# Input terms and weight splits beside the first recurrence tile, weight maxima beside the second attention

## The reference, cut to what matters

```
x = x + attn(cond(x, cond_2048, Wq, Wk, Wv, b), Wq2, Wk2, Wv2, Wo)
gi = x @ W_ih + b_ih                       # input terms of all 256 rows
for each row t:                            # h starts as cond_2048, 8 x 512
    gh = h @ W_hh + b_hh
    r, z = sigmoid(i_r + h_r), sigmoid(i_z + h_z)
    n = tanh(i_n + r * h_n)
    h = (1 - z) * n + z * h
...
h1 = silu(einsum('td,ehd->teh', hs, w1) + b1)      # 8 experts, 352 hidden
out = einsum('ted,te->td', einsum('teh,edh->ted', h1, w2) + b2, comb)
x = x + out
```

## Time and profile before

| | |
|---|---|
| median of 3 runs | 2149.39 us (2143.58 to 2150.28) |
| the profiled execution | 2148.9 us |
| its span, first to last instruction | 2146.8 us |
| TensorE matmul, weight load busy | 1933.3 us (90%), 1687.2 us (79%) |
| VectorE, ScalarE, GpSimd busy | 1346.2 us (63%), 936.4 us (44%), 115.5 us (5%) |
| mean granted TensorE clock | 0.947 |

### The profile page before, as it was taken

How to read it: one execution, slowest core, us unless ns; L and a number is a source line. 1 busy time by engine, 2 the same in 40 slices (tenths; PEclk the granted TensorE clock), 3 DMA queues, 4 the chain that set the end, 5 groups by cost and what they waited for, 6 DMA issues and landing times.

```text
span 2146.8 us, 82157 instructions
## 1 busy us (share of the span) xinstructions
PE 1933.3 (90%) x34302; PEld 1687.2 (79%) x34302; DVE 1346.2 (63%) x5134; ACT 936.4 (44%) x3370; POOL 115.5 (5%) x189
## 2 busy tenths in 40 slices
PE   5889989989998695976689999999999999999999
PEld 3677677677675574866579989989899899898998
DVE  4566665665666107955567776676767766767664
ACT  1355445545545221223335444455454444554443
POOL 0021021021011220000000000000000000000000
PEclk9999999999999897986679999999999999999999
DMA  6000000000000471220000000000000000000000
GB/s 259 1 1 0 0 0 0 0 0 0 0 0 2 152 254 57 74 72 12 9 18 18 18 13 18 18 28 4 28 18 18 13 18 18 28 4 28 4 13 11
DMA packets 54435, 66.14 MB, mean 31 GB/s; under 512 B 4928, under 2 KB 46272, under 8 KB 53104
## 3 DMA queue, kind: packets, MB, share of 16 engines
q1 hardware_dynamic: 50608, 46.96, 6.5%
q0 software_dynamic: 3520, 14.69, 2.2%
HBM read 44.83 MB, written 16.81 MB: 29 GB/s over the span
## 4 chain that ended last, share of the span: by engine, by line
PE 46%; DVE 7%; issue 2%; ACT 1%; DMA 0%; DVEq 0%; ACTq 0%
PE ps L1339 26%; PE ps L1294 10%; PE ps L1273 10%; DVE dh L1470 1%; ACT nn L1390 1%; DVE hn L1463 1%; DVE dh L1476 1%; DVE nxt L1479 1%; DVE nxt L1482 1%; DVE tn L1447 1%; DVE rn L1459 1%; PE ps L1326 0%; DVE h L1480 0%; DVE ns L1472 0%; DVE tb L1556 0%
## 5 line engine op out<-in xcount | busy, mean ns | idle before, releaser
L1339 PE MATMUL ps<-nxt,whf 128*128 128x32 f16 x24576 | 660.5, 177 | 79.3 <-DVE nxt L1482 73.2
L1339 PEld LDWEIGHTS ps<-nxt,whf 128*128 128x128 f16 x24576 | 650.7, 96 | 99.4 <-DVE nxt L1482 88.2
L1390 ACT ACTIVATE rz<-s,sc 128x32 f32<-128x32 f32 x512 | 164.7, 322 | 469.0 <-DVE s L1447 467.8
L1273 PE MATMUL ps<-cur,w1f 128*128 128x256 f16 x2112 | 274.0, 275 | 0.0
L1294 PE MATMUL ps<-hh,w2f 128*128 128x256 f16 x2112 | 265.8, 273 | 0.0
L1294 PEld LDWEIGHTS ps<-hh,w2f 128*128 128x128 f16 x2112 | 205.6, 98 | 23.7
L1447 DVE TENSOR_REDUCE s<-ps 128x32 f32<-128x64 f32 x512 | 114.9, 224 | 165.5 <-PE ps L1339 163.3
L1273 PEld LDWEIGHTS ps<-cur,w1f 128*128 128x128 f16 x2112 | 199.5, 98 | 23.1
L965 PE MATMUL ps<-x1T,wi 128*128 x768 | 175.6, 392 | 21.4 <-DMA wi<-in_W_ih 14.1
L965 PEld LDWEIGHTS ps<-x1T,wi 128*128 128x128 f32 x768 | 150.5, 197 | 46.2 <-issue 24.0
L471 PE MATMUL ps<-kz,rot 128*128 128x256 f32 x512 | 158.0, 391 | 0.0
(11 more groups left out here) (205 smaller groups left out, 2811.2 us busy)
## 6 DMA issues: line engine op xcount, KB each, us to landing
gi_d<-stage SPq DMA_DIRECT2D x96, 128.0 KB, 1.7
gi<-gi_d SPq DMA_DIRECT2D x16, 768.0 KB, 4.9
w1f<-in_w1T POOLq DMA_DIRECT2D x4, 1408.0 KB, 8.7
xall<-in_x SPq DMA_DIRECT2D x4, 1024.0 KB, 9.1
x1T<-in_xT SPq DMA_DIRECT2D x1, 4096.0 KB, 21.9
w2f<-in_w2T POOLq DMA_DIRECT2D x8, 512.0 KB, 4.6
out<-x1T SPq DMA_DIRECT2D x8, 512.0 KB, 3.2
wi<-in_W_ih SPq DMA_DIRECT2D x1, 3072.0 KB, 11.9
```

The costliest lines, as they stand in the source:

```text
L1273: last = nc.tensor.matmul(ps[:, 6 + n % 2, 0:TT], w[:, wp, i % NHC * P:(i % NHC + 1) * P], cur[:, k, hq, :, :].rearrange("p s b -> p (s b) ...
L1339: last = nc.tensor.matmul(ps[:, bank, g * WIDE * 2 * B:(g + 1) * WIDE * 2 * B], whp[:, k, w, q, g * P:(g + 1) * P], h, start=False, stop=( ...
L1390: nc.scalar.activation(o.rearrange("p g b -> p (g b)"), i_.rearrange("p g b -> p (g b)"), func, scale=scale).then_inc(done, 1)
```

## The change

The block `prepare` is gone. Its parts are put into the second attention and into the recurrence block.

In the second attention SyncE loads the small operands and, for each batch, four pieces of weights (of w1 and w2 1408 columns each, of W_hh and W_ih 768 each) into a buffer `seen` of two slots. VectorE takes their maxima between `light` and `lcol` (in the last batch after the second pass), and after each batch the maximum of that batch in x1T. The loads of W_ih and W_hh follow in SyncE's list into the space of the first attention's output and of the projection weights. The hardware loops over batches are written out.

At the start of the recurrence block TensorE makes the input terms of tile 0 in f32 as before, 12 groups; VectorE makes the scales; ScalarE makes the high halves of W_hh, W_ih and of x for tile 1 and evicts the 12 groups straight into `gi`; VectorE makes the low halves.

Beside the 32 steps of tile 0 then go: the input terms of tiles 1 to 7, 84 units (`UNITS`) of 12 f16 matmuls of 256 columns, in halves of 6 (`HALF_AT`), evicted in the next step's first gap (`EVICT_AT`) to a `stage` of two slots and stored to `gi_d` by SyncE; the halves of x for tiles 2 to 7 (`XS_AT`, `XL_AT`); and w1 and w2 in 46 pieces of up to 512 columns, which GpSimd loads into a ring `wring` of three slots, with the high half on ScalarE after the seeds (`WHI_AT`) and the low half on VectorE after the step's state (`WLO_AT`). From step 32 on the steps and the feed-forward hold the same instructions on other addresses; the selector is loaded at step 32, and b2 is scaled at steps 34 and 35.

```diff
+        shared = sb(ctx, "shared", [P, SHARED])
+        hT = shared[:, HT_AT:HT_AT + KD * B * S].rearrange("p (k b s) -> p k b s", k=KD, b=B)
+        w3 = shared[:, 0:3 * KD * D].rearrange("p (w k n) -> p w k n", w=3, k=KD)
+        small = Small(ctx, sb)
...
+                for b in range(B):
+                    for j, (_, src, width) in enumerate(to_see(ins, b)):
+                        if b or j >= 2:
+                            sp.wait_ge(v_seen, 4 * b + j - 1)
+                        sp.dma_start(seen[:, j % 2, 0:width], src).then_inc(d_seen[j % 2], 16)
+                sp.wait_ge(c_hb, B)
+                sp.wait_ge(p_qk, 2 * B)
+                sp.dma_start(shared[:, WI_AT:WI_AT + KD * G3].rearrange("p (k n) -> p k n", k=KD),
+                             ins["W_ih"].rearrange("(k p) n -> p k n", p=P)).then_inc(d_wi, 16)
+                sp.wait_ge(p_v, B + 1)
+                sp.dma_start(shared[:, WH_AT:WH_AT + KD * G3].rearrange("p (k n) -> p k n", k=KD),
+                             ins["W_hh"].rearrange("(k p) n -> p k n", p=P)).then_inc(d_wh, 16)
...
+                def maxima_of_weights(b):
+                    for j, (m, _, width) in enumerate(to_see(ins, b)):
+                        dve.wait_ge(d_seen[j % 2], 16 * (2 * b + j // 2 + 1))
+                        maximum(m, b, seen[:, j % 2, 0:width]).then_inc(v_seen, 1)
...
+                    if more:
+                        maxima_of_weights(b)
...
+                    else:
+                        dve.wait_ge(d_small, 16 * 9)
+                        dve.wait_ge(d_b1, 16 * len(PIECES))
+                        maxima_of_weights(b)
+                        maximum(M_H, 0, small.h32[:, :, :])
+                        maximum(M_GW, 0, small.gw[:, :, :])
+                        maximum(M_B1, 0, small.b1[:, :])
+                        maximum(M_B2, 0, small.b2[:, :])
...
-                with dve.Fori(0, B - 1) as b:
+                for b in range(B - 1):
                     batch(b, True)
+                    dve.wait_ge(v_x, (b + 1) * KD + 1)
+                    maximum(M_X, b, x1T[:, :, :, b])
                 batch(B - 1, False)
+                dve.wait_ge(v_x, B * KD + 1)
+                maximum(M_X, B - 1, x1T[:, :, :, B - 1]).then_inc(v_mx, 1)
+                dve.wait_ge(v_mx, 1)
...
+def to_see(ins, b):
+    w1 = ins["w1T"].rearrange("r (a n) -> (r a) n", a=2)
+    w2 = ins["w2T"].rearrange("h e d -> (h e d)").rearrange("(r n) -> r n", n=NHC * P)
+    whh = ins["W_hh"].rearrange("r (a n) -> (r a) n", a=2)
+    wih = ins["W_ih"].rearrange("r (a n) -> (r a) n", a=2)
+    return [(m, w[b * P:(b + 1) * P, :], w.shape[1])
+            for m, w in ((M_W1, w1), (M_W2, w2), (M_WHH, whh), (M_WI, wih))]
...
-                def tiles(t0, t1):
-                    with pe.Fori(t0, t1) as t:
...
-                                last = nc.tensor.matmul(
-                                    ps[:, q % 4, 0:TT], wi[:, k, q * P:(q + 1) * P],
-                                    x1T[:, k, bass.ds(t * SPT, SPT), :].rearrange("p s b -> p (s b)"),
-                                    start=(k == 0), stop=(k == KD - 1))
...
-                def split(f32, s, width):
-                    t = tmp[:, 0:width]
-                    half = f32.bitcast(F16)
-                    step(nc.vector.tensor_scalar(t, f32, sc[:, s:s + 1], None, ALU.mult))
-                    step(nc.vector.tensor_copy(half[:, 0:width], t))
-                    step(nc.vector.tensor_tensor(half[:, width:2 * width], t, half[:, 0:width], ALU.subtract))
-                for k in range(KD):
-                    split(whf[:, k, :], S_WHH, G3)
-                for k in range(KD):
-                    for a in range(2):
-                        split(w1f[:, k, a, :], S_W1, NHC * P)
-                for c in range(NHC):
-                    split(w2f[:, c, :], S_W2, 2 * D)
-                step(nc.vector.tensor_scalar(bhs[:, :], bgi[:, 1, 2 * KD:NQ], sc[:, S_SEED:S_SEED + 1], None, ALU.mult))
...
+UNITS = (NT - 1) * NQ
+HALF_AT = [1 + n * 30 // (2 * UNITS) for n in range(2 * UNITS)]
+EVICT_AT = [x + 1 for x in HALF_AT[1::2]]
+XS_AT = []
+for _f in range(2, NT):
+    _free = HALF_AT[2 * NQ * (_f - 2) - 1] + 1 if _f > 2 else 0
+    XS_AT += [_free, _free + 1]
+XL_AT = [x + 1 for x in XS_AT]
+W_PIECES = [("w1", k, c, min(D, NCH * P - c)) for k in range(KD) for c in range(0, NCH * P, D)] + \
+           [("w2", c, 0, D) for c in range(NCH)]
+WHI_AT = [1 + n * 29 // len(W_PIECES) for n in range(len(W_PIECES))]
+WLO_AT = [x + 1 for x in WHI_AT]
+WRING = 3
...
+def landed(piece):
+    return 16 * sum(W_DMAS[piece % WRING:piece + 1:WRING])
...
+                for now in range(SPT):
+                    for u in here(EVICT_AT, now):
+                        sp.wait_ge(a_gi, u + 1)
+                        t, q = 1 + u // NQ, u % NQ
+                        sp.dma_start(gi_d[:, q, t * SPT:(t + 1) * SPT, :].rearrange("p s b -> p (s b)"),
+                                     stage[:, u % 2, :]).then_inc(d_st[u % 2], 16)
+                    if now % (SPT // 2) == SPT // 2 - 1:
+                        for j in range(2):
+                            sp.wait_ge(d_st[j], 16 * NQ // 2)
+                        load_when_read(0, now // (SPT // 2))
+                sp.wait_ge(p_gi, UNITS)
+                sp.dma_start(sel32, ins["table"][:, T_ALL:]).then_inc(d_sel, 16)
...
+                for p, (w, k, c, width) in enumerate(W_PIECES):
+                    slot = p % WRING
+                    if p >= WRING:
+                        pool.wait_ge(a_w, p - WRING + 1)
+                        pool.wait_ge(v_w, p - WRING + 1)
+                    if w == "w1":
+                        pool.dma_start(wring[:, slot, 0:width], ins["w1T"][k * P:(k + 1) * P, c:c + width])\
+                            .then_inc(d_ws[slot], 16)
+                    else:
+                        for p0, rows, e, h in w2_parts(k):
+                            pool.dma_start(wring[p0:p0 + rows, slot, :], ins["w2T"][h:h + rows, e, :])\
+                                .then_inc(d_ws[slot], 16)
...
+                def gi_half(u, half):
+                    t, q = 1 + u // NQ, u % NQ
+                    if half == 0:
+                        if u < 4:
+                            pe.wait_ge(a_g0, NQ)
+                        else:
+                            pe.wait_ge(a_gi, u - 3)
+                        if u == 0:
+                            pe.wait_ge(a_sp, 2 * KD)
+                            pe.wait_ge(v_sp, 2 * KD)
+                        if q == 0:
+                            pe.wait_ge(a_xs, 2 * t)
+                            pe.wait_ge(v_xs, 2 * t)
+                    for k in range(2 * half, 2 * half + 2):
+                        for m, (wp, hq) in enumerate(((0, 0), (0, 1), (1, 0))):
+                            last = nc.tensor.matmul(ps[:, 4 + u % 4, 0:TT], wip[:, k, wp, q * P:(q + 1) * P],
+                                                    xs(t)[:, k, hq, :, :].rearrange("p s b -> p (s b)"),
+                                                    start=(k == 0 and m == 0), stop=(k == KD - 1 and m == 2))
+                    if half:
+                        last.then_inc(p_gi, 1)
...
+                pe.wait_ge(d_wi, 16)
+                first_tile_gi(0)
+                first_tile_gi(1)
+                pe.wait_ge(v_a, 1)
+                nc.tensor.transpose(ps[0:NM, 0, 0:P], mxa[:, :], ident).then_inc(p_a, 1)
+                first_tile_gi(2)
+                pe.wait_ge(v_a, 3)
+                nc.tensor.matmul(ps[:, 3, 0:NM], ones9, dg9[:, :], start=True, stop=True).then_inc(p_a, 1)
+                for q in range(3, NQ):
+                    first_tile_gi(q)
...
+                def x_high(f, j):
+                    high(xs(f)[:, 2 * j:2 * j + 2, 0, :, :].rearrange("p k s b -> p k (s b)"),
+                         x1T[:, 2 * j:2 * j + 2, f * SPT:(f + 1) * SPT, :].rearrange("p k s b -> p k (s b)"),
+                         S_X, a_xs)
+                def evict(u):
+                    act.wait_ge(p_gi, u + 1)
+                    if u >= 2:
+                        act.wait_ge(d_st[u % 2], 16 * (u // 2))
+                    nc.scalar.activation(stage[:, u % 2, :], ps[:, 4 + u % 4, 0:TT], ACT.Identity,
+                                         bias=bsum[:, u % NQ:u % NQ + 1], scale=sc[:, S_UNX:S_UNX + 1])\
+                        .then_inc(a_gi, 1)
+                def beside_first_tile(now):
+                    for n in here(XS_AT, now):
+                        f = 2 + n // 2
+                        if n >= 2:
+                            act.wait_ge(p_gi, NQ * (f - 2))
+                        else:
+                            act.wait_ge(v_sp, 2 * KD)
+                            act.wait_ge(p_g0, NQ)
+                        x_high(f, n % 2)
+                    for p in here(WHI_AT, now):
+                        act.wait_ge(d_ws[p % WRING], landed(p))
```

(54 more changed lines are left out.)

528 lines of the change are left out of this document (274 added, 254 removed).

## The result

The changed kernel takes 2066.11 us (median of 4 runs, 2063.97 to 2067.77) against 2148.73 (4 runs) of the kernel before: a ratio of 0.9621, 95% interval 0.9604 to 0.9638. The forecast was 2060, range 2015 to 2110. The profiled execution took 2065.38.

What follows compares the result with a forecast made beforehand. No single engine was full throughout between second attention and first recurrence step; tile 0 alone had free TensorE time. Start 756.5 plus tile 0 240 plus 1061.5 gave span 2058, with 2.1 around it 2060 us; range 2015 to 2110.

Steps and rivals of the forecast that it cites:

- the last term: From tile 0's end to the span's end: same instructions on other addresses, so it stays 1061.5 us.
- The cover in attention: Second attention: four maxima fit VectorE's 7.74 us idle between `light` and `lcol`, nearly; cost +3 us, bounds 0 to +14.
- The start: First recurrence step at 756.5 us, 191.5 earlier, after W_hh lands at 736, ScalarE's 19.3 and seeds' 1.2; bounds 748 to 778.
- Tile 0: First 32 recurrence steps with the added work: 213 plus 22 for late pieces plus 5 for clock, 240 us against 137.3.
- rival (B): Stores and loads hidden, TensorE alone sets tile 0 at 196 us: total 2016, or 2038 with late waits; chance 0.22.
- Late pieces: Tile 0: five weight pieces with one step of slack make ScalarE wait, 4.4 us each, 22 in all (15 to 30).
- The third eviction's wait: Tile 0, steps with three evictions: third waits for the first's store to free its `stage` slot; step 6.85 us over TensorE's 6.34.
- rival (C): Stores in tile 0 land at 3.9 us as beside heavy loads: +41, total 2101; chance with a mild D 0.21.
- The clock: Start of tile 0: one slow step and part of a second at the lower TensorE clock, +5 us.
- signs of being wrong: Tile 0 steps exceed 8 us, a wait stands at every weight piece, or the first step starts after 780.
- Rival (D): Ring of weight pieces bounds tile 0, slower than before from tile 0 = 335 us on; chance in full 0.04.
- page's rule: GpSimd weight loads: fit gives 2.6 us per 256 KB, total 2054; port rule warns VectorE can block GpSimd's descriptor writes.

Runs made afterwards that it cites:

- The later loads: Changed kernel with the loads of W_ih and W_hh issued only behind the attention's last product: 2070.97 us, ratio 0.9660.
- both waits taken away: Changed kernel with three staging slots and five ring slots until piece 39: 2003.76 us, ratio 0.9337; tile 0 192.0 us.

## Why the prediction was right, step by step

**Direction and mechanism.** The total came out 6 us above the forecast, and that is luck in part: the start was 7.7 us early and tile 0 13.7 late. The stage of the f32 input terms (857 to 943) is gone from the path and tile 0 took the work, at a price far below what preparing lost: right. So was the last term, 1061.0 for 1061.5.

**The cover in attention** held; +1.5 us in place of +3.

**The start** came 7.7 us early. The order in SyncE's queue was right, and the issue to 1 us once attention's smaller price is allowed for, but W_hh was there at 731.16 and not at 736 (4.8 us: 1.5 of attention's price, the rest in the landing, 20.4 us after its issue), ScalarE's list took 17.1 and not 19.3 us (neighbours in it overlap: its instructions alone add up to some 19.3), and the seeds 0.5 and not 1.2. The later loads show that the place in the queue sets it, but of W_ih as well as W_hh: the scales stand behind W_ih and were done only 0.7 us before W_hh was there.

**Tile 0** is the step that was mis-sized: 253.7 for 240, and its terms miss by more than their sum, in both directions. TensorE alone (rival (B)'s 196 less 5 for the clock, 191) was right: 192.0 with both waits taken away. From there the runs give 5.2 for late pieces (197.2 - 192.0), 39.3 of idle time and 17.2 of clock for the store waits: 253.7.

"Late pieces", 22 in the forecast (its own 5.9 - 1.3 would give 4.6 each, 23), are those 5, or 2 to 7 in tile 0 and 7 to 9 in the total without the third slot. There were eleven such waits, of 2.7 us in the mean, and not five; most lie beside products that TensorE still has to do, and the forecast had queued all of each onto the next step. Where the wait outlasts the products, as in the step of 12.2 us, TensorE stands at a PSUM bank. In the price of one piece, GpSimd's issue took 0.54 us and not 0.1, for which the prediction names no row.

The third eviction's wait, 213 - 191 = 22, is those 39: a store beside the piece loads held its slot 3.64 us in the step of 7.84, not 0.15 + 1.7 + 0.5. The forecast chose the value near the quiet row because less would move; but a piece's load lies where the stores are, and that is rival (C)'s mechanism, at a part of its price.

"The clock", +5, is 17 us (13 on the input-term products alone: 130.4 for 117.0 to 117.9). The forecast let the clock rise once and stay. It took the new tile 0 as filled to nearly nine tenths, which is 191 of 213; against its own 240 it is eight tenths, and 206.6 of 253.7 is what was measured. Idle gaps pulled the clock down again and again: in stretches of 16 us from 764 on it lay between 0.81 and 1.00.

One of the forecast's signs of being wrong came: steps of tile 0 exceed 8 us, 20 of 32, so their length of 6.3 to 7 was wrong though the total was not. Without both waits they take 4.0 to 7.5.

**Rival (D)** is out: with three ring slots a third stage slot brings tile 0 to 197.2. That the bank behind the eviction keeps TensorE waiting (7.5 us in three waits) was not priced. It belongs to the late pieces: it is gone with five ring slots, though the store waits stay, and 4.1 us of it are left with three stage slots and late pieces.

**Neither page's rule would have come nearer.** The loads of 256 KB landed in 3.1 (w1) and 3.8 us (w2), in the median. The estimate from the fit in the Trainium skill, DMA: Bandwidth & Descriptors, "Anatomy of one DMA — SWDGE (gpsimd) path", was 2.6, below both. On the ports, no run shows GpSimd held up for long: with five ring slots one piece wait of 1.7 us was left beside a VectorE that was busy 105.8 of 246.3 us.

## What to carry to other kernels

A wait that stands in front of a recurrence's gate should be counted twice, once as the wait and once as the clock that TensorE loses by standing idle; one more buffer slot there was worth two thirds of what the whole change had brought. A wait at the end of a step, beside products that TensorE still has to do, costs little until they run out: ask of each wait what TensorE has left to do. Where a store's landing gates compute, price it beside the loads of the same stretch, and look at its slowest landings as well as the median.

## What the runs showed of the hardware

TensorE's granted clock in tile 0 was lower where TensorE stood idle longer at the same matmuls: 0.98 with 3.6 and 7.8 us idle, 0.96 with 24.6, 0.90 with 47.1, 0.82 with 98.3, a mean between the levels of 1.2 and 2.4 GHz. The total of the idle time is not all of it: with 220 useless products in the gaps the clock was 0.98 at 27.2 us idle, and ScalarE's waits nearly stayed. The busy time of the same useful matmuls went from 188.4 to 225.1 us. The Trainium skill, TensorE: Matmul & The Clock Gate, "A second HAM failure mode: psum-queue depth-cycling", tells of a kernel whose frequent short idle stretches between groups of matmuls made the clock swing between its two levels. These runs agree, with gaps of about 2 us (39.5 us in 21 waits for the new state).

Stores of 128 KB landed beside 256 KB loads in a median of 2.4 us (2.8 with five ring slots) and at most 5.1 (5.3), without the loads in 2.3 and 3.6. Taking the loads away was worth 25.7 us of tile 0 with the clock's part in it; which share of that is the slowest landings' is not shown.
